# Turning the next graph's x between the aggregations, with query and values around the third layer's outputs, in a four-layer graph network

## What is computed

```python
# x: (8, 1024, 128), adj: (8, 1024, 1024)
def L0(x):                       # attention over all nodes (the adjacency is the mask)
    q, k, v = x @ Wq.T + bq, x @ Wk.T, x @ Wv.T + bv
    scores = q @ k.T / sqrt(128) + (1 - adj) * -10000
    return softmax(scores) @ v
def L1(x):                       # mean over the neighbours, linear, leaky ReLU
    out = (adj / adj.sum(-1, keepdims=True)) @ x @ W.T + b
    return where(out >= 0, out, 0.01 * out)
def L2(h):                       # graph attention, 4 heads of 32, softmax over i
    Wh = (h @ W)                 # per head: s_i = Wh . a_src, s_j = Wh . a_dst
    e = leaky(s_i[:, None] + s_j[None, :], 0.2); e[adj == 0] = -1e9
    return softmax(e, over i).T @ Wh
def L3(H):                       # symmetric normalisation with self loops
    A1 = adj + eye; d = rsqrt(A1.sum(-1))
    return ((A1 * d[:, None] * d[None, :]) @ H) @ B
x = ln(x + L0(x)); x = ln(x + L1(x)); x = ln(x + L2(x)); x = ln(x + L3(x))
```

## Time and profile before

| | |
|---|---|
| median of 3 runs | 960.63 us (956.34 to 961.43) |
| the profiled execution | 956.48 us, span 954.7 us |
| PE / DVE / ACT / POOL busy | 88% / 76% / 62% / 34% |
| mean granted TensorE clock | 0.963 of full speed |
| matmuls / loads of weights | 10841 / 10856 |
| HBM over the span | 62 GB/s |

### The profile page before, as it was taken

One profiled execution on the slowest core, in us unless ns is written; L12 is line 12 of the kernel. 1 busy time (PEld: TensorE's weight loads), 2 busy tenths in 40 slices (PEclk: granted clock), 3 DMA queues, 4 the chain that ended last, 5 costly groups with the idle time before them and its releaser, 6 DMA issues.

```text
span 954.7 us, 25283 instructions
## 1 busy us (share of the span) xinstructions
PE 837.2 (88%) x10841; PEld 681.5 (71%) x10856; DVE 730.2 (76%) x1635; ACT 588.1 (62%) x668; POOL 327.5 (34%) x335
## 2 busy tenths in 40 slices
PE   5988999799997999989997999979999799964874
PEld 3664799557985689747895579856797478952873
DVE  4438877788868898689877788678887898765975
ACT  1664685667765776567756667657765678545503
POOL 2022511724044520716117250354206161064504
PEclk9998999999999999999999999999999999986997
DMA  9723117921178124660268211781237602600270
GB/s 185 129 63 64 52 47 91 154 69 45 55 104 154 46 83 69 115 133 6 90 92 158 64 45 47 103 164 46 67 69 127 137 6 68 91 0 23 68 91 22
DMA packets 166463, 77.39 MB, mean 81 GB/s; under 512 B 136624, under 2 KB 154160, under 8 KB 166352
## 3 DMA queue, kind: packets, MB, share of 16 engines
q1 hardware_dynamic: 156864, 58.48, 31.7%
q0 software_dynamic: 8448, 16.78, 10.0%
q10 hardware_dynamic: 1040, 0.52, 0.2%
HBM read 54.66 MB, written 4.33 MB: 62 GB/s over the span
## 4 chain that ended last, share of the span: by engine, by line
PE 29%; issue 27%; DVE 24%; POOL 9%; ACT 7%; DVEq 0%; POOLq 0%; ACTq 0%
PE ring L1202 8%; PE Z L1224 7%; DVE x L847 5%; DVE cmat L811 3%; POOL rstd L472 3%; PE ring L1256 3%; ACT steps L655 2%; PE ring L1200 2%; DVE meanvar L840 2%; DVE ring L756 2%; ACT maskb L592 2%; DVE x L928 2%; POOL cmat L527 2%; DVE x L933 2%; DVE x L931 2%
## 5 line engine op out<-in xcount | busy, mean ns | idle before, releaser
L655 ACT ACTIVATE steps<-sjrow,steepsi 128x1024 bf16<-128x1024 f32 x248 | 266.7, 1138 | 87.8 <-DVE cmat L811 66.2
L811 DVE TENSOR_TENSOR cmat<-steps,adj 128x1024 f16<-128x1024 bf16 x180 | 152.9, 893 | 20.0 <-ACT steps L655 18.0
L1256 PE MATMUL ring<-vparts,cmat 128*128 128x66 bf16 x4416 | 143.7, 194 | 16.8 <-DVE vparts L956 7.7
L1256 PEld LDWEIGHTS ring<-vparts,cmat 128*128 128x128 f16 x4416 | 141.3, 98 | 18.1 <-issue 7.9
L1224 PEld LDWEIGHTS Z<-vv,probs 128*128 128x128 f32 x1024 | 123.6, 192 | 31.6 <-issue 17.2
L1202 PE MATMUL ring<-qT,xT 128*128 128x512 f32 x256 | 139.5, 627 | 0.0
L1224 PE MATMUL Z<-vv,probs 128*128 128x129 f32 x1024 | 125.0, 275 | 9.0 <-ACT probs L662 9.0
L662 ACT ACTIVATE probs<-ring 128x1024 f32<-128x1024 f32 x64 | 65.1, 1017 | 63.7 <-PE ring L1202 63.7
L756 DVE CUSTOM_DVE_ANT_0 ring<-ring,maskb 128x1024 f32<-128x1024 f32 x64 | 78.4, 1228 | 31.7 <-PE ring L1140 19.1
L527 POOL TENSOR_TENSOR cmat<-cmat,ident 128x1024 f16<-128x1024 f16 x8 | 17.1, 2142 | 238.4 <-DMA cmat<-adj 238.4
L1237 PE MATMUL ring<-vparts,adj 128*128 128x132 bf16 x1536 | 94.0, 222 | 0.9 <-POOL vparts L507 0.9
(11 more groups left out here) (126 smaller groups left out, 1373.7 us busy)
## 6 DMA issues: line engine op xcount, KB each, us to landing
adj<-in_adj_dram POOLq DMA_DIRECT2D x16, 1024.0 KB, 13.0
sjrow<-sj_rows SPq DMA_DIRECT2D x31, 512.0 KB, 4.0
out_dram<-x SPq DMA_DIRECT2D x16, 256.0 KB, 2.4
x<-in_x_dram SPq DMA_DIRECT2D x7, 512.0 KB, 4.1
adjT<-adj SPq DMA_TRANSPOSE x64, 3.5
cmat<-adj SPq DMA_TRANSPOSE x64, 4.4
x<-in_x_dram ACTq DMA_DIRECT2D x1, 512.0 KB, 4.2
small<-in_a_dram SPq DMA_DIRECT2D x1, 128.0 KB, 9.5
```

Source lines behind the costliest of these rows:

```text
L655: act.activation(steps[:, n % STEPS, :], sjrow[:, h % 2, :], ACT.Relu, bias=steepsi[:, t, h:h + 1], scale=STEEP).then_inc(step_made, 1)
L811: dve.tensor_tensor(c_of[:, t, :], steps[:, n % STEPS, :], adjs[o.parity][:, t, :], ALU.min)\
L1256: last = pe.matmul(s[:, jt, 0:VW], c_of[:, t, jt * P:(jt + 1) * P], vparts[:, t, h, part, :], start=t == 0 and part == 0, stop=t == T - 1 ...
```

## The change

- The order of the products is one list over all graphs (`SEQ`), and `claim` looks three places back in it.
- x of graph g + 1 is turned on PE between the two aggregations of step g, its query made ahead of, and its values behind, the second half of layer 3's output.
- x2T goes to Z, no longer to the ring.
- ACT reads xT after widening tile 3 for layer 3, and at the end of the step makes mask 0, reads q, makes mask 1, reads v, and makes masks 2 and 3 of the next graph. Masks 4 to 7 stay behind sj.
- DVE casts xT ahead of layer 1's output, and qT between the halves of x2's normalisation, with layer 3's output on both sides.
- POOL makes the degrees ahead of the diagonal, and adds the diagonal in two instructions, six blocks and two; the older graph's normalisation (L481, L484) stays on POOL.
- Minimum 7 of head 0 comes ahead of the older graph's last normalisation.
- In the last step the adjacency is turned at the start, into the free adjacency buffer, and its diagonal is added ahead of the values, which get a buffer of their own.

The diff, cut to its core:

```diff
+            return [(name, graph, k) for name, k in names] if 0 <= graph < NB else []
+
+        seq = []
+        if n == 0:
+            seq += of(0, ("xT", 0), ("q", 0), ("v", 0)) + of(0, *[("s", t) for t in range(5)])
+        elif n < NB:
+            seq += of(n, ("s", 0), ("s", 1), ("s", 2)) + of(n - 1, ("wh", 0)) + of(n, ("s", 3)) \
+                + of(n - 1, ("wh", 1), ("sj", 0)) + of(n, ("s", 4))
+        else:
+            seq += of(n - 1, ("wh", 0), ("wh", 1), ("sj", 0))
+        for t in range(T):
+            seq += of(n, ("st", t))
+            if t < 3:
+                seq += of(n, ("s", 5 + t))
+        masks, c = [("mask", 0), ("mask", 1)], [("c", h) for h in range(H)]
+        seq += of(n - 1, *(masks + c if n < NB else c[:1] + masks + c[1:]))
+        seq += of(n, ("out1", 0)) + of(n + 1, ("xT", 0)) + of(n, ("out1", 1)) + of(n - 1, ("out3", 0)) \
+            + of(n + 1, ("q", 0)) + of(n - 1, ("out3", 1)) + of(n + 1, ("v", 0))
+        return seq
+
+    SEQ = [group for n in range(NB + 1) for group in groups_of(n)]
+    PLACE = {group: n for n, group in enumerate(SEQ)}
+    assert len(PLACE) == len(SEQ)
...
 
-            def turn_older(o):
-
-                sp.wait_ge(full["c"], o.count(2 * H, 4))
+            def turn_older(kind, o):
+
+                if kind == "last":
+                    sp.wait_ge(c_made, o.count(H * T))
+                    sp.wait_ge(full["mask"], o.count(2))
+                    sp.wait_ge(turned_older, o.count(16 * 6))
+                    sp.wait_ge(turned_last, o.count(16 * 2))
+                else:
+                    sp.wait_ge(full["c"], o.count(2 * H, 4))
                 for t in range(T):
-                    sp.dma_start_transpose(adjT_of_older[:, :, t * P:(t + 1) * P], adjs[o.parity][:, t, :])\
-                        .then_inc(turned_older, 16)
+                    sp.dma_start_transpose(OLDER_T[kind][:, :, t * P:(t + 1) * P], adjs[o.parity][:, t, :])\
+                        .then_inc(turned_older if t < 6 else turned_last, 16)
 
             def step(kind, g):
                 o = g.before()
                 if kind != "last":
                     turn_adj(g)
+                if kind == "last":
+                    turn_older(kind, o)
...
@@ -413,8 +430,8 @@
 
                     sp.wait_ge(y_made[0], g.count(2, 2))
                     sp.dma_start(x0[:, :, :], x_v[number(Graph(g.base + 1))]).then_inc(x_in, 16)
-                if kind != "first":
-                    turn_older(o)
+                if kind == "full":
+                    turn_older(kind, o)
 
             program(step)
             store(Graph(NB - 1))
...
-            def add_diagonal(g):
-                pool.wait_ge(turned_older, g.count(16 * T, 16 * T))
-                blocks = diagonal_blocks(adjT_of_older)
-                pool.tensor_tensor(blocks, blocks, ident16[:, :].unsqueeze(1).broadcast_to([P, T, P]), ALU.add)\
-                    .then_inc(diag_added, 1)
+            def add_diagonal(kind, g):
+                for n, (turned_, at, blocks) in enumerate(((turned_older, 0, 6), (turned_last, 6, 2))):
+                    pool.wait_ge(turned_, g.count(16 * blocks, 16 * blocks))
+                    diagonal = diagonal_blocks(OLDER_T[kind], at, blocks)
+                    pool.tensor_tensor(diagonal, diagonal, ident16[:, :].unsqueeze(1).broadcast_to([P, blocks, P]),
+                                       ALU.add).then_inc(diag_added, 1)
...
                     bias_x0(g)
+                if kind == "last":
+                    add_diagonal(kind, o)
                 if kind != "first":
                     split_values(kind, o)
                     if kind == "last":
                         rstd_of(3, o.before())
                 if kind != "last":
                     rstd_of(0, g)
+                    degree_of(g)
                 if kind != "first":
-                    add_diagonal(o)
+                    if kind == "full":
+                        add_diagonal(kind, o)
                     rstd_of(2, o)
                     if o.base < NB - 2:
 
                         pool.wait_ge(full["mask"], o.count(2, 2))
                         pool.wait_ge(c_made, o.count(H * T, H * T))
                         load_adj(Graph(o.base + 2))
-                if kind != "last":
-                    degree_of(g)
-                if kind != "first":
                     for k in range(2):
                         pool.wait_ge(split3, o.count(6, 3 * k + 1))
                         norm_apply(2, o, x3, k)
...
                                 step_tile(kind, o, n_step)
                             made += PACE[n]
+                following = Graph(g.base + 1)
                 if kind == "first":
                     widen(kind, g, "agg1", range(T))
                     take_sums("agg1", g, agg1T)
-                    make_maskb(Graph(1), range(4, T))
+                    for n, name in enumerate(("xT", "q", "v")):
+                        take_group(kind, following, name, 0)
+                        make_maskb(following, ([4], [5], [6, 7])[n])
                     return
                 for n in range(made, len(STEP_TILES[kind])):
                     step_tile(kind, o, n)
                 if kind == "full":
                     widen(kind, g, "agg1", range(T))
+                    widen(kind, o, "agg3", [0])
                     take_sums("agg1", g, agg1T, [0])
-                    widen(kind, o, "agg3", [0])
+                    widen(kind, o, "agg3", [1, 2])
                     take_sums("agg1", g, agg1T, [1])
-                    widen(kind, o, "agg3", range(1, T))
+                    widen(kind, o, "agg3", [3])
+                    if following.base < NB:
+                        take_group(kind, following, "xT", 0)
+                    widen(kind, o, "agg3", range(4, T))
                 else:
                     widen(kind, o, "agg3", range(T))
-                take_sums("agg3", o, agg3T)
+                for k in range(2):
+                    take_sums("agg3", o, agg3T, [k])
+                if kind == "full" and following.base < NB:
+                    make_maskb(following, [0])
+                    take_group(kind, following, "q", 0)
+                    make_maskb(following, [1])
+                    take_group(kind, following, "v", 0)
+                    make_maskb(following, [2, 3])
 
             program(step)
...
                 if kind == "first":
@@ -1038,11 +1078,11 @@
                     take_part(kind, o, 0, 1)
                     mins(kind, o, 0, range(4, 7))
                     take_part(kind, o, 1, 1)
+                    mins(kind, o, 0, range(7, T))
                 if kind == "full" and finish:
                     norm_apply(3, o.before(), x3, 0)
                     norm_apply(3, o.before(), x3, 1)
                 if kind == "full":
-                    mins(kind, o, 0, range(7, T))
                     mins(kind, o, 1)
                 norm_apply(0, g, x1, 0)
...
                     last_heads(kind, o)
+                following = Graph(g.base + 1)
+                more = following.base < NB
+                if more:
+                    cast_x(following)
                 for k in range(2):
                     layer1_out(kind, g, k)
                     norm_stats(1, g, x2, k)
-                final = g.base == NB - 1
-                if kind == "full" and not final:
-
+                if kind == "full" and more:
                     layer3_out(kind, o, 0)
+                norm_apply(1, g, x2, 0)
+                if more:
+                    cast_q(following)
+                if kind == "full" and more:
                     layer3_out(kind, o, 1)
-                norm_apply(1, g, x2, 0)
                 norm_apply(1, g, x2, 1)
-                if final:
+                if not more:
...
+            def claim(name, g, k):
+
+                n = PLACE[name, g.base, k]
                 if n >= SLOTS:
-                    (was, j), of = ORDER[kind][n - SLOTS], g
-                elif kind == "first":
-                    return slot(kind, name, k)
-                elif g.base == 1:
-                    (was, j), of = ORDER["first"][n - SLOTS], g.before()
-                else:
-                    (was, j), of = ORDER["full"][n - SLOTS], g.before()
-                if was in OLDER:
-                    of = of.before()
-                if was == "out3":
-                    pe.wait_ge(y_made[3], of.count(2, j + 1))
...
@@ -1141,13 +1178,15 @@
                                      start=True, stop=True)
                 last.then_inc(full["s"], 1)
 
-            def head_inputs(kind, g, name, k):
-                o = g.before()
+            def head_inputs(kind, o, name, k):
                 if name == "x2T":
                     pe.wait_ge(normed[1], o.count(2, 2))
-                    transposes(kind, o, g, "x2T", x2)
+                    pe.wait_ge(read["agg1"], o.count(2, 2))
+                    if o.base > 0:
```

(17 more changed lines are left out.)

186 lines of the change are left out of this document (96 added, 90 removed).

## The result

| | before | after |
|---|---|---|
| median of the runs | 961.03 us (956.34 to 962.62, 4 runs) | 930.50 us (928.95 to 937.87, 4 runs) |
| profiled execution, span | 956.48 us, 954.7 us | 928.95 us, 927.1 us |
| mean granted clock | 0.963 | 0.963 |

The ratio of the times is 0.9705, with a 95% interval of 0.9652 to 0.9757. The change gains about 3%, where the prediction had 5%: 930.5 us against 912, just outside the upper end of its range of 901 to 930.

A forecast was written before the change was run, and what follows sets the result against it. DVE's and ACT's chain was taken to bound the boundary between graphs, besides a mid-step wait; 33.7 + 1.5 + 3.4 + 1.3 + 5.0 - 0.3 = 44.6 us gave 912 us, range 901 to 930.

The forecast's parts named there:

- the boundary: Between two graphs: x2 ready earlier and x, q, v no longer behind it; scores start 5.1 us earlier per step.
- GpSimd in DVE's way: Rival: diagonal and x3's normalisation on GpSimd stretch DVE's instructions, 2 us in seven places; 926 us, chance 0.12.
- a packed boundary can only help: TensorE's clock: less idle time ahead keeps it from falling to 1.2 GHz; 1.3 us booked.
- Early degree: Degree ahead of the diagonal: DVE's 3.25 us wait goes, not booked apart since the turned x's cast is late next.
- Graph 0 to 1: First boundary: DVE waits for xT ahead of layer 1's output; loss of 0.3 us, bounds -1 and +2.
- The last graph's boundary: No x turned there; early degrees and diagonal in parts give x2 3.4 us, bounds 1.5 and 4.
- The exponential's wait: Mid-step, minimum 7 ahead of the normalisation removes TensorE's 1.50 us wait, six times: 9.0 us.
- The end: Last step: adjacency turned at the start, diagonal ahead of the values; 5.0 us in all, bounds 3 and 6.
- The 0.9 us that were added there for the clock: Last aggregation: clock gain from less idle time ahead of it, part of the end's 5.0 us.
- the rival that would have made it slower: Adjacency load holds ACT's mask 0 ahead of q, all six boundaries losing about 8.3 us; 966 us, chance 0.04.
- The first part of the diagonal: First six blocks need not wait for the last two turned tiles; diagonal ends 1.5 us earlier.
- TensorE's own work: 103.1 us of a steady step; the forecast step of 105.5 us stands 2.4 above it.

The follow-up runs named there:

- b5: a4 with, in the first step, the cast of x behind layer 1's first half, and the last diagonal behind x2's normalisation; 895.91 us, ratio 0.9336.
- c2: Changed kernel with GpSimd's normalisation of x3 held until both splits and the cast of x are done; 909.56 us, ratio 0.9474.
- a3: Changed kernel with GpSimd's addition of the value bias to the next x held until x2 is normalised; 915.29 us, ratio 0.9527.
- b4: Kernel before with only the degree ahead of the diagonal and minimum 7 ahead of the normalisation, nothing turned early; 936.08 us, ratio 0.976.
- b6: b4 with the bias later and x3's normalisation behind both splits, still nothing turned early; 931.17 us, ratio 0.97.
- a4: Changed kernel with both GpSimd jobs later: the value bias and the normalisation of x3; 897.88 us, ratio 0.9365.
- a1: Changed kernel with the degree back behind the load of the adjacency; 933.36 us, ratio 0.9727.
- c1: b5 with the degree back behind the load of the adjacency; 914.28 us, ratio 0.9529.
- a0: Changed kernel run again, unaltered, as the control; 932.98 us, ratio 0.9724 to the kernel before.
- b1: Changed kernel with minimum 7 of head 0 back behind the older graph's last normalisation; 941.51 us, ratio 0.9822.

## Why the prediction was wrong, and where it was right

**The step that failed** is the boundary, "followed from the end of the first aggregation at 504.2", 5.1 us in each of six steps. Its order of events was right, and so was TensorE's part in it: the queries were early, and v, which waited 1.44 us for its slot, ended at 512.45, as forecast (512.4). The step that failed in it is the one that put the overlap of x3's normalisation with DVE's splits at nothing. The risk was named as the second rival, "GpSimd in DVE's way", priced at 926 us with a chance of 0.12, and set aside with the sentence "DVE has about 2 us of waiting there for the deviations, which swallow it; I book nothing". The wait lies ahead of the first split and the stretch falls on the second, where DVE has nothing to wait for; its wait for the deviations was 0.68 us in this boundary. Against the rows of b5 the second split takes 2.4 us more, its subtraction 0.7 and the cast of x 0.8. Moving that normalisation alone (c2) gives back 23 us, more than the 18.5 that were missing, and lands at 909.6 us beside the forecast of 912.

The bias is another matter. The normalisation of x2 takes 2.1 us more in this boundary than in b5, and a3 gives back 18 us, but most of that was in the kernel before as well (73.8 against 63.1 us for the group) and so in the forecast's price, 3.67 us for both halves; they took 4.3 here. Nor did the forecast price every instruction as if it ran alone: its 1.42 us for parts of layer 1's output is a stretched row, and these took 0.69.

Another part is the clock. Of the six stretches 8.6 us are missing: 3.8 and 2.5 of them in the two at less than full clock. In the window of 612 to 632 it was 0.83. From the timeline there:

```profile
623.02 1.91 PE L1148 MATMUL Z<-identf,x 128*128 128x128 f32 x8
```

This group takes 1.09 us in the boundary before it. That is the 1.2 GHz level instead of 2.4. TensorE had stood 1.69 us for v's slot and 1.94 us for the cast of q; in the boundary before it stood 1.44 and 1.93 and kept its clock, so what tips it isn't shown. Nor do the overlaps alone decide it: b4, with an overlap on the split, has one stretch below 1.00, and b6, with none, has three. What the profiles do show is that all six stretches are at 1.00 in a3, c2, a4 and b5. The Trainium skill ("TensorE: Matmul & The Clock Gate", The HAM clock gate) has the throttled state as the default one. By that, the trace agrees in part: the level fell behind waits of TensorE, but not behind nearly equal ones. The prediction's "a packed boundary can only help" stood on the boundary being packed, which it wasn't.

**Early degree.** It was booked as hidden behind the cast of x, and was worth nothing as made (a1). That was luck: the reason is another one, and without the overlap it is worth 2.6 us a boundary (c1).

**Graph 0 to 1** was booked at a loss of 0.3 us, from -1 to +2. In the profile above the first stretch is 5.25 us longer, in the same kernel's second profile (a0) 1.04. Most of the 5.25 isn't the change's. The first aggregation of graph 0 already starts 1.3 us later (0.2 in a0), behind DVE's wait for the first adjacency (6.3 us, 5.5 in a0, 4.9 before). Counted from there x2 is turned 1.4 us later than before in both profiles: that is the order's price, DVE waiting for the turned x where it had layer 1's output to do. What follows is the clock, from the changed kernel's two profiles:

```profile
73.52 0.69 DVE L1030 CAST qxb<-xT 128x1024 bf16<-128x1024 f32 x1 [6.91 <-ACT xT L599]
...
85.65 1.97 PE L1148 MATMUL Z<-identf,x 128*128 128x128 f32 x8 [0.82 <-DVE x L881]
```

```profile
84.61 1.09 PE L1148 MATMUL Z<-identf,x 128*128 128x128 f32 x8 [1.51 <-DVE x L881]
```

In the seven profiles that share this first step the transposed scores of graph 1 come at 90.6 to 96.3, in the three with the old one (before, b4, b6) at 90.6 to 93.1. So a loss beyond the booked bounds isn't shown.

**The last graph's boundary** was to give 3.4 us and, with the exponential's 1.5, 4.9. It gave 2.2 (1.8 in a0). The diagonal of the last step now falls on the second half of x2's normalisation, 2.78 us in place of 1.1, which is 1.7 of the 2.7 us missing:

```profile
830.37 2.26 POOL L545 TENSOR_TENSOR adj<-adj,ident 128x768 f16<-128x768 f16 x2
830.43 2.78 DVE L881 TENSOR_SCALAR x<-x,meanvar,rstd 128x128 f32<-128x128 f32 x4 [0.47 <-POOL rstd L489]
```

**Right.** The exponential's wait: 1.5 us in each of six steps; b1 gives it back with 8.5 to 11 us and its own row. The end: 5.5 us of the 6.3 booked with the clock. Its last aggregation starts at 906.53, 5.15 us behind the last product that TensorE had, a little over the forecast ("4 to 5 us"), and 10.24 before. The 0.9 us that were added there for the clock did not come: the first 16 products of this aggregation take 6.80 us, where they took 5.48 before. The adjacency's load delayed nobody, so the rival that would have made it slower didn't show. The first part of the diagonal: 0.8 to 1.1 us measured in b5, 1.5 booked.

**Wrong to the other side.** With the overlaps gone the six stretches of b5 are 102.2 to 103.8 us, not 105.5. I held back there: the boundary's chain had 2.4 us above TensorE's own work. A window over one step of b5 shows TensorE busy for 100.6 of 103.8 us, at the full clock:

```profile
398.30:502.10 103.80, 100.60 (x1358) 83.19 (x1357) 88.92 (x202) 74.04 (x85) 42.49 (x41) 1.00 0.47 93
```

The 103.1 us that the prediction took for TensorE's own work is mostly that work at a lower clock: its window has 0.98, and the two other windows of the earlier trace rows, at 1.00, have 101.0 and 101.6. The remaining 0.4 to 1.0 us above b5 I can't place. The best version is b5, 895.9 us, 6.6% under the kernel before, with the same instructions as the changed one.

## What to carry to other kernels

When a re-ordering moves an engine's work beside another's, price the stretched instruction too: look in the trace of before for the same pair overlapping, and put a price on it in the sum, even when one row is all there is. Here the price is what is left of the other engine's instruction, not a factor on one's own (next section). An edit that measures as nothing may be a gain that another part ate; test it again after the other part is mended. And compare the busy time of each engine at an unchanged number of instructions first, since it showed this cause in one row. Profile the same kernel twice before explaining a stretch that is a few microseconds longer: here the first one differed by 4.2 us between two profiles of the same kernel.

## What the runs showed of the hardware that I had not expected

How much GpSimd stretches DVE, and which of its instructions. In the boundary between graphs 4 and 5, four tensor_scalar instructions of 128 x 128 fp32 went from 1.12 to 3.51 us (L904) and to 3.16 (L881), a cast of 128 x 1024 from fp32 to bf16 from 0.69 to 1.53, a difference of two operands of 128 x 512 from 0.69 to 1.42. In b5 layer 1's output from PSUM (L967, 1.12 us) ran beside GpSimd's L498 and was not stretched, while its last sum of two SBUF operands (L972) was, 1.41. Single instructions of the changed kernel show more than the groups do:

```profile
495.74 1.03 DVE L904 TENSOR_SCALAR rest<-x,meanvar,drstd 128x128 f32<-128x128 f32 x1
496.68 1.21 DVE L904 TENSOR_SCALAR rest<-x,meanvar,drstd 128x128 f32<-128x128 f32 x1
...
510.76 2.40 DVE L881 TENSOR_SCALAR x<-x,meanvar,rstd 128x128 f32<-128x128 f32 x1
```

A tensor_scalar takes 0.34 us alone, and each of these ends just behind an instruction of GpSimd: L881 at 513.16 (L464 at 513.08), the second L904 at 497.88 (L498 at 497.79). The subtraction ends at 501.16 and the cast at 502.61, 0.55 us behind GpSimd's at 500.61 and 502.06. These distances are the same within 0.01 us in all six boundaries of the changed kernel. So the instruction is not slowed in proportion: it ends when GpSimd's has ended, and one long instruction of GpSimd costs DVE its whole remainder. The first L904 ends at 496.77, and what ended just ahead of it, at 496.72, is GpSimd's issue of the adjacency's load (L447), so 0.7 of the 2.4 us on the split stand beside that. In b5 the split beside the same issue took its 1.12 us, so this part stays open. A tensor_scalar beside GpSimd's small instructions (128 x 4, L489, 1.1 us) kept its 0.34. The small head instruction that takes 0.29 alone took 1.63 beside the diagonal:

```profile
488.72 1.68 POOL L545 TENSOR_TENSOR cmat<-cmat,ident 128x768 f16<-128x768 f16 x1 [22.53 <-DMA cmat<-adj]
...
488.91 1.63 DVE L935 TENSOR_TENSOR small<-small 128x132 f32<-128x132 f32 x1
```

It too ends when GpSimd's instruction has ended (490.54 and 490.40). The Trainium skill ("GPSIMD Engine Reference", Specifications) says that GpSimd's SBUF interfaces are shared with VectorE, with contention for DVE instructions that have two SBUF inputs or run in a 2-port performance mode. By that, the trace agrees for the instructions with two SBUF operands and for the row from PSUM. For the tensor_scalar and the cast, with one SBUF tensor each, it would have to be the mode. The cast's pace fits: 512 more columns cost it 0.26 us (0.43 to 0.69), while 380 more cost the two-operand instructions 0.40 (0.29 to 0.69), so it does about twice as many elements in a microsecond. The tensor_scalar ran in one size only, so for it no run here shows the mode.
